# Mean layer of a graph network: edge features split in half tiles, residual and bias formed on POOL

## The chip, the cores and the metric

The kernel runs on one core of one Trainium2 chip. The metric is device microseconds (us) of one execution. Before the change it took 2363.88 us (median of 3 runs, 2360.2 to 2365.95).

## The reference

Four graph layers follow each other over 3125 nodes of 128 features and 103,125 edges that are sorted by target node. The change is in the second one, the mean layer, which the kernel overlaps with work for the fourth:

```
# layer 1 (mean aggregation), then residual and layer norm
agg = segment_sum(x[col], row, n) / max(degree, 1)
h   = relu(agg @ W1.T + b1)
x   = layernorm(x + h @ W2.T + b2)
# layer 3 needs, per target node, the sum of its edges' 16 features
segment_sum(edge_attr_16, dst, n)
```

## The kernel before

The nodes are held as 25 tiles of 128 (`TILES`), and a strip is 5 tiles (`STRIPS` = 5). `k.C` holds the matrix of edge counts, so that an aggregation is a matrix product. `mean_layer` (L877) does 5 strips x 25 tiles = 125 steps `(i, t)`. In each, PE transposes five 128x128 blocks of `k.C` (`turn`, L1115), ACT copies them from PSUM to `cs` (L1085), and PE adds 8 matmuls into `pA` and `pD` (`add`, L1129).

The edge sums run in the same steps. An edge tile has 36 chunks of 128 edges (`EC`), cut into 4 batches of 9 chunks (`EB`); there are 100 batches, in the steps t = 1 to 6 and 11 to 24 of each strip (`with_batch`). For batch n:

- SP waits for `lower` of batch n-2, loads an address register and issues the DMA of `feat[n % 2]`, 72 KB (`load_batch`, L940); before the first batch of a tile it also issues the targets `dst` (L931).
- The f32 features are split into three bf16 parts in `eparts[n % 2]`. ACT casts the high part (`high_part`, L1073, needs the DMA and the end of batch n-2 on PE); POOL subtracts it, giving `left` (L1049); ACT casts the middle part (`middle_part`, L1077); POOL subtracts that, giving the low part (L1051).
- DVE compares targets with places and writes the one-hot matrices `hot[n % 2]` (`match`, L1010, needs the end of batch n-2). It reads two operands from SBUF, as do POOL's subtractions.
- PE does 9 matmuls (`batch`, L1142), which need `hots` and `low` of batch n. After each fourth batch DVE takes the sum out of PSUM (L1015, L1016).

ACT, PE, DVE and SP run their queues in the order of the steps. ACT's and PE's work for a strip's end hangs in the next strip's steps: DVE's `mean(i-1)` at t = 1 (L974, a reciprocal of 4.15 us at L976, L978), PE's `first` after t = 2 (L1152), ACT's `hidden` at t = 4 (L1063), PE's `second` after t = 6 (L1158), DVE's `finish(i-1)` behind the match of t = 6. `finish` adds the bias b2 to the PSUM result (L986), then the residual x (L988), both into y, and normalizes (L707 to L714). The x of a strip is loaded by SP at t = 12 (L961), the old strip is stored at t = 20 (L946).

Of the kernel before, what the change touches and what calls it, by code (L numbers as in the profile page):

```python
# [26 lines left out]
P = 128  # L27
N_NODES = 3125
N_EDGES = 103125
D = 128  # L30
# [48 lines left out]
LIVE = N_NODES + 1  # L79
RISE = 2.0 ** 40  # L80
CHUNKS = ((0, 6), (6, 12), (12, 18), (18, TILES))
V_PARTS = tuple((lo, lo + PERIOD) for lo in range(0, TILES, PERIOD))
# [55 lines left out]
def mid(row, n):  # L138

    p, w = row.shape  # L140
    return row.unsqueeze(1).broadcast_to([p, n, w])
# [735 lines left out]
def mean_layer(nc, a, k, parts):  # L877
# [3 lines left out]
    with ExitStack() as ctx:  # L881
# [5 lines left out]
        cs = m.sb("cs", [P, CS, SW], BF16)  # L887
        x, y, out = (m.sb(n, [P, STRIP, D], F32) for n in ("x", "y", "out"))
        sq, w = out, out[:, 0:2, :]
# [3 lines left out]
        places = m.sb("places", [P, P, EG], BF16)  # L893
        feat, left = m.sb("feat", [P, 2, EB, FE], F32), m.sb("left", [P, 2, EB, FE], F32)
        dst, key = m.sb("dst", [P, 2, EC], I32), m.sb("key", [P, 2, EC + 1], BF16)
        eparts = m.sb("eparts", [P, 2, EB, ER], BF16)
        hot = m.sb("hot", [P, 2, (EB + 1) // EG, P, EG], BF16)
# [6 lines left out]
            m.sem(n) for n in ("turned", "cs_ready", "cs_used", "agg_out", "deg_out"))  # L904
        aggT_ready, p1, hT_ready, p2, added = (m.sem(n) for n in ("aggT_ready", "p1", "hT_ready", "p2", "added"))
        chain, var, std, normed, stored = (m.sem(n) for n in ("chain", "var", "std", "normed", "stored"))
        feat_in, dst_in = ([m.sem(f"{n}{s}") for s in (0, 1)] for n in ("feat_in", "dst_in"))
        high, lower, middle, low = (m.sem(n) for n in ("high", "lower", "middle", "low"))
# [9 lines left out]

        def part_of(n, part):
            return eparts[:, n % 2, :, 1 + FE * part:1 + FE * (part + 1)]  # L920

        with nc.Block() as block:
            @block.sync
            def _(sp):
# [8 lines left out]

                def load_batch(n):
                    t, b = divmod(n, HB)
                    if b == 0:
                        load_dst(t)
                    if n > 1:
                        sp.wait_ge(lower, n - 1)
                    sp.dma_start(feat[:, n % 2], a["edge_attr"][bass.ds(edges(t), EC * P), :]  # L940
                                 .rearrange("(p c) f -> p c f", c=EC)[:, b * EB:(b + 1) * EB, :]
                                 ).then_inc(feat_in[n % 2], 16)

# [8 lines left out]
                sp.dma_start(b2[:, :], a["b2_1"].partition_broadcast(P)).then_inc(consts, 16)  # L952
                load_batch(0)
                load_batch(1)
                sp.dma_start(x[:, :, :], strip_of(k.x1, 0)).then_inc(loaded, 16)
                for n, (i, t) in enumerate(with_batch):
                    if n + 2 < len(with_batch):
                        load_batch(n + 2)
# [9 lines left out]
            def _(dve):  # L968
# [11 lines left out]
                def finish(i):  # L980
                    link = Chain(dve, chain, i * (1 + NORM_LINKS))
                    dve.wait_ge(p2, i + 1)
                    if i:
                        dve.wait_ge(normed, i)
                    dve.wait_ge(loaded, i * 16 + 16)
# [10 lines left out]
                    normalize(link, act_link, dve, y[:, :, :], sq[:, :, :], st, out[:, :, :]).then_inc(normed, 1)  # L996
                    assert link.n == 1 + NORM_LINKS, link.n

# [43 lines left out]
            def _(pool):  # L1042
                pool.iota(places[:, :, :], [[1, P], [0, EG]], base=0, channel_multiplier=0,
                          allow_small_or_imprecise_dtypes=True).then_inc(made, 1)
                for n in range(len(with_batch)):
                    pool.wait_ge(high, n + 1)
                    if n > 1:
                        pool.wait_ge(low, n - 1)
                    pool.tensor_tensor(left[:, n % 2], feat[:, n % 2], part_of(n, 0), ALU.subtract).then_inc(lower, 1)  # L1049
                    pool.wait_ge(middle, n + 1)  # L1050
                    pool.tensor_tensor(part_of(n, 2), left[:, n % 2], part_of(n, 1), ALU.subtract).then_inc(low, 1)  # L1051
                pool.wait_ge(cs_used, STRIPS * TILES)
# [5 lines left out]
            def _(act):  # L1058
# [9 lines left out]

                def high_part(n):
                    act.wait_ge(feat_in[n % 2], 16 * (n // 2 + 1))  # L1070
                    if n > 1:
                        act.wait_ge(chunks, n - 1)
                    nc.scalar.activation(part_of(n, 0), feat[:, n % 2], ACT.Copy).then_inc(high, 1)  # L1073

                def middle_part(n):
                    act.wait_ge(lower, n + 1)
                    nc.scalar.activation(part_of(n, 1), left[:, n % 2], ACT.Copy).then_inc(middle, 1)  # L1077
# [26 lines left out]
            def _(pe):  # L1104
# [30 lines left out]
                def batch(n):  # L1135
                    t, b = divmod(n, HB)
                    pe.wait_ge(hots, n + 1)
                    pe.wait_ge(low, n + 1)
                    if t and b == 0:
                        pe.wait_ge(sums_out, t)  # L1140
                    for c in range(EB):
                        ins = pe.matmul(pE[:, :], hot[:, n % 2, c // EG, :, c % EG], eparts[:, n % 2, c, :],  # L1142
                                        start=b == 0 and c == 0, stop=b == HB - 1 and c == EB - 1,
                                        skip_group_check=True)
                    ins.then_inc(chunks, 1)
# [1472 lines left out]
```

## Time and profile before

| | |
|---|---|
| time, median of 3 runs | 2363.88 us |
| profiled execution, span | 2364.9 us, mean granted TensorE clock 0.898 |
| engines over the whole span | PE 76%, DVE 61%, ACT 43%, POOL 40% |
| mean layer, first hot to last output | about 569 to 857 us |
| its steps, 570 to 838 us | PE busy 222.96 us, DVE 178.95, POOL 152.23, ACT 144.64 of 268 |

Each row of a timeline gives the start in us from the span's start, how long the instruction took, its engine, line, operation, output and input tile, and in brackets how long the engine had been idle and what ended that. "SPq" rows are DMA issues by SP; a DMA's landing is later. A table of windows gives the busy time of each engine in a stretch, with the granted clock (1.00 is 2.4 GHz, 0.50 is 1.2 GHz). In a group of lines, the numbers behind the bar are busy us, mean ns of one instruction, and the idle time of the engine just before them, with what ended it. Where an engine waited for two things, the one that is named isn't always the one that came last: the ends of both have to be compared.

### The profile page before, as it was taken

The numbers are of one execution on the slowest core, as the hardware profiler recorded it, in microseconds if no ns is written. First come the engines' busy times: TensorE is split into PE (matmuls) and PEld (weight loads), VectorE is DVE, ScalarE is ACT, GpSimd is POOL, SyncE is SP. The second block draws the span as 40 slices with busy tenths as digits, with TensorE's granted clock in tenths as the row PEclk, the third lists the DMA queues.
The fourth block names the chain that finished last, engine by engine and source line by source line (L and its number), as shares of the span: only waits on it lengthen the run. The fifth ranks groups of instructions, "written<-read, shape, count | busy, mean of one in ns | idle before, by whom it ended". The sixth has DMA issues, their size and how long they took to land. (4 is left out here: it accounts for less than half of the span.)

```text
span 2364.9 us, 63669 instructions
## 1 busy us (share of the span) xinstructions
PE 1804.0 (76%) x24559; PEld 1430.7 (60%) x24674; DVE 1433.6 (61%) x2262; ACT 1017.2 (43%) x1655; POOL 956.2 (40%) x664
## 2 busy tenths in 40 slices
PE   4699998744888832788888886249907999999996
PEld 1699998733556522677777776149904555555553
DVE  6799999535676743799999997548760111110213
ACT  1455555302555511888889896237600110110100
POOL 0899889314555530888888770000031000000000
PEclk9899999956999966899999999669958999999998
DMA  1100000021111112111111100410020000000001
GB/s 50 38 13 14 14 12 11 11 66 44 34 43 42 42 33 63 35 41 37 37 37 37 37 33 7 116 60 12 12 85 18 9 7 8 6 9 4 15 14 43
DMA packets 93856, 73.97 MB, mean 31 GB/s; under 512 B 22862, under 2 KB 84055, under 8 KB 93505
## 3 DMA queue, kind: packets, MB, share of 16 engines
q1 hardware_dynamic: 90279, 67.88, 10.0%
q0 software_dynamic: 3328, 2.56, 0.6%
q8 instruction: 182, 2.98, 0.5%
q14 instruction: 67, 0.55, 0.1%
HBM read 51.57 MB, written 18.84 MB: 30 GB/s over the span
## 5 line engine op out<-in xcount | busy, mean ns | idle before, releaser
L2136 ACT ACTIVATE branch_mask<-branch_row,att_att 128x3126 bf16<-128x3126 f32 (+1 forms) x208 | 460.8, 2288 | 45.9 <-DMA branch_row<-dst_row 31.4
L429 POOL DMA_INDIRECT swp_slab<-records,e_rows x100 | 335.7, 3357 | 90.8 <-POOLq L110 56.1
L2213 PE MATMUL branch_acc<-branch_v,branch_mask 128*128 128x102 bf16 (+1 forms) x5000 | 297.8, 213 | 62.4 <-DVE branch_mask L2163 41.1
L2169 DVE TENSOR_TENSOR branch_mask<-branch_mask,k_C 128x3126 bf16<-128x3126 bf16 (+1 forms) x208 | 313.8, 1556 | 16.4 <-ACT branch_mask L2136 15.7
L2213 PEld LDWEIGHTS branch_acc<-branch_v,branch_mask 128*128 128x128 bf16 (+1 forms) x5000 | 254.6, 100 | 89.1 <-DVE branch_mask L2163 45.4
L2471 DVE SCALAR_TENSOR_TENSOR sage_y<-sage_pO,k_rdeg,sage_b 128x128 f32<-128x128 f32 x125 | 34.6, 344 | 449.7 <-PE sage_pO L2398 449.4
L862 PE MATMUL sage_pA<-k_C,k_x_parts 128*128 x2175 | 299.3, 294 | 4.9 <-issue 1.0
L862 PEld LDWEIGHTS sage_pA<-k_C,k_x_parts 128*128 x2250 | 166.4, 98 | 133.4 <-issue 3.3
L353 PE MATMUL swp_pw<-swp_key_hot,swp_low_hot 128*128 128x100 bf16 x1568 | 201.2, 217 | 31.8 <-DVE swp_key_hot L347 31.6
L2452 ACT ACTIVATE sage_aggT<-sage_pA 128x640 f32<-128x640 f32 x25 | 17.6, 703 | 463.5 <-PE sage_pO L2398 368.4
L353 PEld LDWEIGHTS swp_pw<-swp_key_hot,swp_low_hot 128*128 128x128 bf16 x1568 | 180.4, 119 | 39.2 <-DVE swp_key_hot L347 38.1
L356 PE MATMUL swp_pw<-swp_key_hot,swp_low_hot 128*128 128x50 bf16 x3136 | 201.3, 192 | 0.0
L862 PE MATMUL sage_pA<-k_C,sage_parts 128*128 x1460 | 198.3, 293 | 2.2
L356 PEld LDWEIGHTS swp_pw<-swp_key_hot,swp_low_hot 128*128 128x128 bf16 x3136 | 192.1, 117 | 0.0
L2202 PE MATMUL branch_acc<-branch_v,k_C 128*128 128x51 bf16 x5000 | 165.9, 187 | 28.9 <-POOL branch_v L2111 16.9
L347 DVE TENSOR_TENSOR swp_key_hot<-swp_key_hot,swp_tab 128x400 bf16<-128x400 bf16 x588 | 178.8, 358 | 0.0
L2202 PEld LDWEIGHTS branch_acc<-branch_v,k_C 128*128 128x128 bf16 x5000 | 143.5, 97 | 41.6 <-issue 22.4
L862 PEld LDWEIGHTS sage_pA<-k_C,sage_parts 128*128 x1500 | 110.1, 97 | 87.6
L1973 PE MATMUL scaled_acc<-scaled_tab,scaled_e 128*128 (+1 forms) x1250 | 142.1, 277 | 9.2 <-DVE scaled_e L1950 9.2
L1010 DVE TENSOR_TENSOR mean_hot<-mean_places,mean_key 128x1280 bf16<-128x1280 bf16 x100 | 120.9, 1222 | 46.4 <-PE mean_pE L1142 46.1
L1973 PEld LDWEIGHTS scaled_acc<-scaled_tab,scaled_e 128*128 128x128 f32 x1250 | 141.9, 194 | 9.5 <-issue 9.5
L842 POOL CAST k_x_parts<-post_out 128x640 bf16<-128x640 f32 x5 | 3.6, 716 | 347.6 <-DVE post_out L714 347.6
(307 smaller groups left out, 3218.0 us busy)
## 6 DMA issues: line engine op xcount, KB each, us to landing
branch_row<-dst_row SPq DMA_DIRECT2D x24, 384.0 KB
mean_feat<-in_edge_attr SPq DMA_DIRECT2D x100, 72.0 KB, 1.9
branch_row<-dst_row SPq DMA_DIRECT2D x8, 411.0 KB
sage_edges<-edgeT SPq DMA_DIRECT2D x25, 127.5 KB
table<-lin_tab SPq DMA_DIRECT2D x5, 340.0 KB, 5.3
branch_tab<-table SPq DMA_DIRECT2D x8, 212.5 KB
att_sums<-branch_mask SPq DMA_DIRECT2D x8, 212.5 KB, 2.3
post_sums<-att_sums SPq DMA_DIRECT2D x5, 340.0 KB, 3.4
```

The costliest lines, as they stand in the source:

```text
L347: ins = dve.tensor_tensor(key_hot[:, :, 1 + f], key_hot[:, :, 0], weight.broadcast_to(shape), ALU.mult)
L353: pe.matmul(out[:, 0:2 * KEYS], low_hot, key_hot[:, 0:2, :].rearrange("p f j -> p (f j)"), start=start, stop=False, skip_group_check=True)
L356: ins = pe.matmul(out[:, KEYS:2 * KEYS], low_hot, key_hot[:, f, :], start=False, stop=f == PARTS, skip_group_check=True)
L429: pool.indirect_dma_start(slab[:, t % 2, j * ROW:(j + 1) * ROW, :].rearrange("p e f -> p (e f)"), None, k.records, bass.IndirectOffsetOnAx ...
L862: ins = pe.matmul(pA[:, lo:hi], parts[:, part, bass.ds(s * STRIP + t, 1), :].rearrange("p a f -> p (a f)"), k.C[:, bass.ds(s * STRIP + t, ...
L1010: dve.tensor_tensor(hot[:, n % 2], places[:, :, :].unsqueeze(1).broadcast_to(shape), of.unsqueeze(2).broadcast_to(shape), ALU.is_equal).th ...
L1973: ins = pe.matmul(acc_tile(j, c), e[:, slot, c * P:(c + 1) * P], one(tab, s), start=isinstance(s, int) and s == 0 and c % per_bank == 0, s ...
L2136: nc.scalar.activation(mask[:, slot(e, s), cols(lo, hi)], row[:, cols(lo, hi)], ACT.Relu, bias=g.att[:, 1, bass.ds(h + s * heads, 1)], sca ...
L2169: dve.tensor_tensor(at[:, cols(lo, hi)], at[:, cols(lo, hi)], k.C[:, s, cols(lo, hi)], ALU.min).then_inc(masked, 1)
L2202: pe.matmul(block_of(e, t)[:, half:2 * half], k.C[:, s, t * P:(t + 1) * P], v[:, s, 2, :, :].rearrange("p r c -> p (r c)"), start=s == 0 a ...
L2213: ins = pe.matmul(block_of(e, t)[0:wide.stop - wide.start], mask[:, slot(e, s), wide], v[:, s, 0:2, :, :].rearrange("p x r c -> p (x r c)" ...
L2471: ins = dve.scalar_tensor_tensor(out=y[:, c, :], in0=pO[:, c * D:(c + 1) * D], scalar=k.rdeg[:, i * STRIP + c:i * STRIP + c + 1], in1=b[:, ...
```

## The change

Within `mean_layer`, four things change.

- Features are fetched and split in groups of two batches (18 chunks, 144 KB): 50 groups in place of 100 batches, so 50 DMAs of features, 100 ACT casts and 100 POOL subtractions of 128x288 in place of 100, 200 and 200 of 128x144. DVE's matches and PE's batches stay 100 of 9 chunks.
- The remainder overwrites `feat` in place (the tile `left` is gone), so the DMA of group g waits for `low` of group g-2 and no longer for `lower`. `feat` has 2 buffers, `eparts` has 3 (`GROUPS`). ACT's high part of group g waits for batch 2(g-3)+1.
- The order is another: ACT casts `high_part(g + 2)` at the odd batch of group g and `middle_part(g + 1)` at the even one, with `high_part(0)`, `high_part(1)` and `middle_part(0)` ahead of the first step. POOL does `lower_part(g + 1)` and then the low part of g.
- POOL adds b2 to x in place (`add_bias`, after group 8 of every 10), and DVE's `finish` has one addition where it had two; y is gone, and x is normalized in place. SP's load of x waits for `normed` in place of `added`.

```diff
-                    if n > 1:
-                        sp.wait_ge(lower, n - 1)
+                    if g > 1:
+                        sp.wait_ge(low, g - 1)
...
-                        sp.wait_ge(added, i)
+                        sp.wait_ge(normed, i)
                         sp.dma_start(x[:, :, :], strip_of(k.x1, i)).then_inc(loaded, 16)
...
-                    link(dve.tensor_tensor(y[:, :, :], flatB[:, 0:SW].rearrange("p (t f) -> p t f", f=D),
-                                           mid(b2[:, :], STRIP), ALU.add))
-                    dve.tensor_tensor(y[:, :, :], y[:, :, :], x[:, :, :], ALU.add).then_inc(added, 1)
+                    dve.wait_ge(residual, i + 1)
+                    dve.tensor_tensor(x[:, :, :], flatB[:, 0:SW].rearrange("p (t f) -> p t f", f=D), x[:, :, :],
+                                      ALU.add).then_inc(added, 1)
...
+                def add_bias(i):
+                    pool.wait_ge(consts, 16 * 4)
+                    pool.wait_ge(loaded, i * 16 + 16)
+                    pool.tensor_tensor(x[:, :, :], x[:, :, :], mid(b2[:, :], STRIP), ALU.add).then_inc(residual, 1)
+
+                def lower_part(g):
+                    pool.wait_ge(high, g + 1)
+                    pool.tensor_tensor(feat[:, g % 2], feat[:, g % 2], part_of(g, 0),
+                                       ALU.subtract).then_inc(lower, 1)
+
+                lower_part(0)
+                for g in range(2 * TILES):
+                    if g + 1 < 2 * TILES:
+                        lower_part(g + 1)
+                    pool.wait_ge(middle, g + 1)
+                    pool.tensor_tensor(part_of(g, 2), feat[:, g % 2], part_of(g, 1), ALU.subtract).then_inc(low, 1)
+                    if g % (HB * STRIP // 2) == HB * STRIP // 2 - 2:
+                        add_bias(g // (HB * STRIP // 2))
...
+                def high_part(g):
+                    act.wait_ge(feat_in[g % 2], 16 * (g // 2 + 1))
+                    if g >= GROUPS:
+                        act.wait_ge(chunks, 2 * (g - GROUPS + 1))
+                    nc.scalar.activation(part_of(g, 0), feat[:, g % 2], ACT.Copy).then_inc(high, 1)
...
                 high_part(0)
+                high_part(1)
+                middle_part(0)
...
-                        middle_part(batch_of[i, t])
-                        if batch_of[i, t] + 1 < len(with_batch):
-                            high_part(batch_of[i, t] + 1)
+                        g, odd = divmod(batch_of[i, t], 2)
+                        if odd and g + 2 < 2 * TILES:
+                            high_part(g + 2)
+                        elif not odd and g + 1 < 2 * TILES:
+                            middle_part(g + 1)
...
-                    pe.wait_ge(low, n + 1)
+                    pe.wait_ge(low, n // 2 + 1)
```

## Rows read from the trace of the kernel before

**Rows 1.** Windows, batches of t = 11 to t = 24 in each strip, with columns.
```profile
core 0: us, PE busy (x) PEld busy (x) DVE busy (x) ACT busy (x) POOL busy (x), PEclk, DMA share, GB/s
592.34:620.72 28.38, 22.77 (x288) 16.20 (x286) 17.17 (x22) 15.82 (x40) 20.76 (x26) 1.00 0.17 37
646.49:673.58 27.09, 22.93 (x288) 16.02 (x287) 18.39 (x24) 15.26 (x38) 21.13 (x26) 1.00 0.25 61
702.29:731.38 29.09, 24.45 (x287) 17.47 (x288) 18.42 (x24) 16.07 (x40) 19.07 (x27) 0.94 0.23 57
757.14:784.26 27.12, 22.94 (x288) 16.10 (x288) 18.25 (x24) 15.25 (x38) 21.27 (x27) 1.00 0.25 61
811.38:837.37 25.99, 22.60 (x281) 16.15 (x282) 16.54 (x22) 15.13 (x37) 19.27 (x26) 1.00 0.24 60
```

**Rows 2.** Timeline, two batches in steady state.
```profile
605.77 0.39 PE L1142 MATMUL mean_pE<-mean_eparts,mean_hot 128*128 128x49 bf16 x9
606.20 1.49 DVE L1010 TENSOR_TENSOR mean_hot<-mean_places,mean_key 128x1280 bf16<-128x1280 bf16 x1 [0.84 <-PE mean_pE L1142]
606.53 1.48 POOL L1051 TENSOR_TENSOR mean_eparts<-mean_left,mean_eparts 128x144 bf16<-128x144 f32 x1 [0.44 <-ACT mean_eparts L1077]
607.97 0.45 POOL L1049 TENSOR_TENSOR mean_left<-mean_feat,mean_eparts 128x144 f32<-128x144 f32 x1
608.16 0.39 PE L1142 MATMUL mean_pE<-mean_eparts,mean_hot 128*128 128x49 bf16 x9 [0.62 <-POOL mean_eparts L1051]
608.59 0.83 DVE L1010 TENSOR_TENSOR mean_hot<-mean_places,mean_key 128x1280 bf16<-128x1280 bf16 x1 [0.89 <-PE mean_pE L1142]
609.17 0.33 SPq L940 DMA_DIRECT2D mean_feat<-in_edge_attr  x1
...
611.05 0.33 ACT L1073 ACTIVATE mean_eparts<-mean_feat 128x144 bf16<-128x144 f32 x1 [0.54 <-DMA mean_feat<-in_edge_attr]
```

**Rows 3.** Timeline, PE's spacing of two batches that nothing holds up.
```profile
576.48 0.39 PE L1142 MATMUL mean_pE<-mean_eparts,mean_hot 128*128 128x49 bf16 x9
...
578.08 0.39 PE L1142 MATMUL mean_pE<-mean_eparts,mean_hot 128*128 128x49 bf16 x9
```

**Rows 4.** Groups of lines, 566 to 858 us.
```profile
L1010 DVE TENSOR_TENSOR mean_hot<-mean_places,mean_key 128x1280 bf16<-128x1280 bf16 x100 | 120.9, 1222 | 46.4 <-PE mean_pE L1142 46.1
L1051 POOL TENSOR_TENSOR mean_eparts<-mean_left,mean_eparts 128x144 bf16<-128x144 f32 x100 | 93.7, 937 | 91.8 <-ACT mean_eparts L1077 91.8
...
L1049 POOL TENSOR_TENSOR mean_left<-mean_feat,mean_eparts 128x144 f32<-128x144 f32 x100 | 61.2, 612 | 27.5 <-ACT mean_eparts L1073 27.0
...
L1073 ACT ACTIVATE mean_eparts<-mean_feat 128x144 bf16<-128x144 f32 x100 | 32.8, 328 | 60.5 <-DMA mean_feat<-in_edge_attr 40.3 <-PE mean_pE L1142 19.7
...
L1098 ACT ACTIVATE mean_aggT<-mean_pA 128x640 f32<-128x640 f32 x5 | 3.5, 704 | 2.0 <-PE mean_pD L1129 2.0
```

**Rows 5.** Timeline, a POOL subtraction of 640 elements in the layer before.
```profile
559.61 1.39 POOL L843 TENSOR_TENSOR gin_rest<-gin_out,x_parts 128x640 f32<-128x640 f32 x1
```

**Rows 6.** DMA issues, 566 to 840 us: count, KB each, median us to landing.
```profile
mean_feat<-in_edge_attr SPq DMA_DIRECT2D x100, 72.0 KB, 1.9
...
x<-mean_out SPq DMA_DIRECT2D x4, 320.0 KB, 2.6
```

**Rows 7.** Timeline, the handover from ACT's cast to POOL's subtraction.
```profile
601.25 0.33 ACT L1073 ACTIVATE mean_eparts<-mean_feat 128x144 bf16<-128x144 f32 x1 [2.95 <-DMA mean_feat<-in_edge_attr]
...
601.66 0.45 POOL L1049 TENSOR_TENSOR mean_left<-mean_feat,mean_eparts 128x144 f32<-128x144 f32 x1 [1.75 <-ACT mean_eparts L1073]
```

**Rows 8.** Timeline, the first two operations of DVE's finish.
```profile
638.60 0.82 DVE L986 TENSOR_TENSOR mean_y<-mean_pB,mean_b 128x640 f32<-128x640 f32 x1 [3.89 <-PE mean_pB L1158]
...
639.45 0.82 DVE L988 TENSOR_TENSOR mean_y<-mean_y,mean_x 128x640 f32<-128x640 f32 x1
```

**Rows 9.** Windows, strip's last batch to t = 6, the shortest and longest of four.
```profile
620.72:636.71 15.99, 12.92 (x149) 9.46 (x150) 12.22 (x13) 9.04 (x22) 7.94 (x13) 1.00 0.12 25
673.58:691.32 17.74, 14.28 (x150) 10.24 (x150) 12.64 (x13) 9.11 (x21) 7.94 (x12) 0.90 0.12 27
```

More of the change, by code:

```diff
@@ L80 @@
 RISE = 2.0 ** 40
+GROUPS = 3
 CHUNKS = ((0, 6), (6, 12), (12, 18), (18, TILES))
@@ L887, in mean_layer @@
         cs = m.sb("cs", [P, CS, SW], BF16)
-        x, y, out = (m.sb(n, [P, STRIP, D], F32) for n in ("x", "y", "out"))
+        x, out = (m.sb(n, [P, STRIP, D], F32) for n in ("x", "out"))
         sq, w = out, out[:, 0:2, :]
@@ L893, in mean_layer @@
         places = m.sb("places", [P, P, EG], BF16)
-        feat, left = m.sb("feat", [P, 2, EB, FE], F32), m.sb("left", [P, 2, EB, FE], F32)
+        feat = m.sb("feat", [P, 2, EC // 2, FE], F32)
         dst, key = m.sb("dst", [P, 2, EC], I32), m.sb("key", [P, 2, EC + 1], BF16)
-        eparts = m.sb("eparts", [P, 2, EB, ER], BF16)
+        eparts = m.sb("eparts", [P, GROUPS, EC // 2, ER], BF16)
         hot = m.sb("hot", [P, 2, (EB + 1) // EG, P, EG], BF16)
@@ L904, in mean_layer @@
             m.sem(n) for n in ("turned", "cs_ready", "cs_used", "agg_out", "deg_out"))
-        aggT_ready, p1, hT_ready, p2, added = (m.sem(n) for n in ("aggT_ready", "p1", "hT_ready", "p2", "added"))
+        aggT_ready, p1, hT_ready, p2, added, residual = (
+            m.sem(n) for n in ("aggT_ready", "p1", "hT_ready", "p2", "added", "residual"))
         chain, var, std, normed, stored = (m.sem(n) for n in ("chain", "var", "std", "normed", "stored"))
-        feat_in, dst_in = ([m.sem(f"{n}{s}") for s in (0, 1)] for n in ("feat_in", "dst_in"))
+        feat_in = [m.sem(f"feat_in{s}") for s in (0, 1)]
+        dst_in = [m.sem(f"dst_in{s}") for s in (0, 1)]
         high, lower, middle, low = (m.sem(n) for n in ("high", "lower", "middle", "low"))
@@ L917, in mean_layer, with part_of @@
         assert len(with_batch) == TILES * HB
-        def part_of(n, part):
-            return eparts[:, n % 2, :, 1 + FE * part:1 + FE * (part + 1)]
+        def part_of(g, part):
+            return eparts[:, g % GROUPS, :, 1 + FE * part:1 + FE * (part + 1)]
         with nc.Block() as block:
@@ L980, in finish @@
                 def finish(i):
[L981 removed]
+                    link = Chain(dve, chain, i * NORM_LINKS)
                     dve.wait_ge(p2, i + 1)
[L983 to L988 removed]
+                    dve.wait_ge(residual, i + 1)
+                    dve.tensor_tensor(x[:, :, :], flatB[:, 0:SW].rearrange("p (t f) -> p t f", f=D), x[:, :, :],
+                                      ALU.add).then_inc(added, 1)
                     dve.wait_ge(added, i + 1)
@@ L995, in finish @@
                         dve.wait_ge(stored, i * 16)
-                    normalize(link, act_link, dve, y[:, :, :], sq[:, :, :], st, out[:, :, :]).then_inc(normed, 1)
-                    assert link.n == 1 + NORM_LINKS, link.n
+                    normalize(link, act_link, dve, x[:, :, :], sq[:, :, :], st, out[:, :, :]).then_inc(normed, 1)
+                    assert link.n == NORM_LINKS, link.n
                 def match(n):
@@ L1044, in _ @@
                           allow_small_or_imprecise_dtypes=True).then_inc(made, 1)
[L1045 to L1051, printed above, removed]
+                def add_bias(i):
[14 more added lines that the diff above has]
+                        add_bias(g // (HB * STRIP // 2))
                 pool.wait_ge(cs_used, STRIPS * TILES)
@@ L1067, in root, with middle_part @@
                     nc.scalar.activation(st[:, 2, :], st[:, 1, :], ACT.Sqrt).then_inc(std, 1)
[L1069 to L1077, printed above, removed]
+                def high_part(g):
[3 more added lines that the diff above has]
+                    nc.scalar.activation(part_of(g, 0), feat[:, g % 2], ACT.Copy).then_inc(high, 1)
+                def middle_part(g):
+                    act.wait_ge(lower, g + 1)
+                    nc.scalar.activation(part_of(g, 1), feat[:, g % 2], ACT.Copy).then_inc(middle, 1)
                 high_part(0)
+                high_part(1)
+                middle_part(0)
                 act.wait_ge(consts, 16 * 4)
@@ L1141, in batch @@
                     for c in range(EB):
-                        ins = pe.matmul(pE[:, :], hot[:, n % 2, c // EG, :, c % EG], eparts[:, n % 2, c, :],
+                        ins = pe.matmul(pE[:, :], hot[:, n % 2, c // EG, :, c % EG], eparts[:, n // 2 % GROUPS, n % 2 * EB + c, :],
                                         start=b == 0 and c == 0, stop=b == HB - 1 and c == EB - 1,
```

20 lines of the change are left out of this document (10 added, 10 removed).

## The prediction, made before the changed kernel was run

> **What bounds the kernel now.** I read the page first (the mean layer is a stage of its own, some 290 of 2364.9 us), then windows of that stage, then its timeline. The changed code runs nowhere else, so only the mean layer can move, unless it leaves the clock or a queue in another state for the next stage.
>
> In the stretch t = 11 to 24 of each strip, which has 14 batches and so 13 spacings, the five strips take 28.38, 27.09, 29.09, 27.12 and 25.99 us, 137.7 in all [rows 1]: 2.12 us a batch, 4.24 a pair. PE, when nothing holds it, needs 1.60 us for a step with a batch [rows 3], 3.20 a pair, and is busy 22.6 to 24.5 us of 26 to 29 [rows 1]. So PE is not quite the bound. The timeline shows what is [rows 2]. The batch at 605.77 ends; DVE's next hot starts 0.43 later and takes 1.49 us. POOL's low part starts at 606.53 and takes 1.48 us where the same kind of subtraction takes 0.45 at 607.97: it ends at 608.01, which is 0.32 behind the hot's end at 607.69. PE's batch follows at 608.16. The reader should see that POOL stands still while DVE runs an operation with two SBUF operands, and that every batch then costs 0.43 + hot + 0.32 + 0.15 us: 2.39 with the 1.49 us hot, 1.72 with the 0.83 us one (608.16 to 609.88 by this sum). The two kinds of hot alternate, and their mean is 1.22 [rows 4]. PE's waits are booked partly on the hot, but the low part ends last.
>
> The supply of features is close behind: ACT's high part waited 40.3 us in all for DMA and 19.7 for PE's batches, by two buffers [rows 4].
>
> **The change: the pace of a group.** The terms of one subtraction of 288 elements: 0.45 us for 144 [rows 2], 1.39 for 640 [rows 5], so by the straight line 0.72; bounds 0.45 (all fixed) and 0.90 (all by size). ACT's cast: 0.33 for 144 and 0.70 for 640 [rows 4], so 0.44; bounds 0.33 and 0.66. The DMA: low or left end to issue 0.75 (608.42 to 609.17), issue to ACT's start 1.88 [rows 2]; a 320 KB DMA lands 0.7 later than a 72 KB one [rows 6], so 144 KB lands 0.2 later, 2.08; bounds 1.88 and 2.58. ACT to POOL 0.08 [rows 7].
>
> Saved work: POOL's subtractions were 200 x 0.45 = 90 us unblocked and become 100 x 0.72 = 72, so 18 us less need of the port that DVE's hots also use; ACT saves 100 x 0.66 - 100 x 0.44 = 22 us. Neither is an engine's full load, so this counts only through what each step waits for.
>
> What decides is the new order. The DMA of group g waits for low(g-2); POOL must do lower(g) before low(g-1); lower(g) needs high(g), which needs the DMA. So one round, low(g-2) to low(g-1), holds a whole DMA and two subtractions in series: 0.75 + 2.08 + 0.44 + 0.08 + 0.72 + 0.72 = 4.79 us for two batches, against 4.24 now. Before, the DMA of batch n waited only for left(n-2), and one such round (0.75 + 1.88 + 0.33 + 0.08 + 0.45 = 3.49) served two batches. The three `eparts` buffers don't help: `feat` has two, and the position of lower ahead of low makes them act as one. ACT waits in its queue at high(g), and the copy `cs` of the next step stands behind it, so PE is starved by the same round.
>
> Then the hots. Measured from the end of a high part (H), copy 0.69 and PE's step put the next batches at H + 2.1 and H + 3.7, the hots that follow them at H + 2.6 and H + 4.2 (0.2 later where DVE first takes sums out). The next lower part is due at H + 4.9. A 1.49 us second hot runs until 5.7 or 5.9 and holds it; a 0.83 one is over or nearly so. A held 144-element operation ended 0.32 behind the hot, 0.13 less than its own 0.45, so a held one of 288 ends about 0.59 behind. The second hot is long in the two groups of one tile and short in the two of the next. Working four groups in a row gives rounds of 4.8, 5.6, 5.1 and 4.8: mean 5.1. I take 5.1 us.
>
> The Trainium skill (SBUF — State Buffer, "SBUF: two separate sides") says that whichever of a two-input DVE operation and a GpSimd operation starts first has the shared ports for the whole instruction and the other fully blocks. The trace agrees, with 1.48 us for a 0.45 us operation. By a strict reading, with the blocked one starting only then, it would need its full 0.72 behind the hot; that would add 0.13 in about half the rounds, 2 us over the layer.
>
> **The change: the sum.** In t = 11 to 24, the second pair follows the first after about 3.4 us (its features were fetched during the strip's tail, but its lower part meets two hots), then five rounds of 5.1 lead to t = 23, then 1.9 to t = 24: 30.8 us. The last strip has no lower part after group 49 and saves 1.9. Five strips: 5 x 30.8 - 1.9 = 152.1, against 137.7: +14.4.
>
> Between a strip's last batch and t = 6 (15.99 to 17.74 us now [rows 9]) DVE's mean with its long reciprocal sets the pace, and the DMA round fits under it. ACT no longer waits there for the batch before last, but larger POOL operations can hold the mean's last product by up to 0.7: -0.4 for each of 4, -1.5; bounds -4 and +3.
>
> `finish` loses its first addition, 638.60 to 639.45, 0.85 us [rows 8]. The hot for t = 11 stands behind it, and at the end the next layer does: 5 x -0.85 = -4.3. The residual is long there: add_bias has about 1.4 us [rows 5] and comes after group 8 of 10, in the 3.3 us in which POOL waits for the next high part; if that cover is gone, it costs up to 1.4 x 5 = 7. Behind its wait for x, loaded ten steps earlier, stand POOL's lower parts. SP's load of x now waits for the end of normalizing, which is also what frees the hot for t = 11, so the feature DMA behind it isn't late; and the 320 KB are in flight before the next feature DMA.
>
> At the start ACT does high(0), high(1) and middle(0) before its first copy, which waits for a lower part under the second hot: some 2.5 us later, most of which the first rounds would have cost anyway: +0.5; bounds 0 and +2.5.
>
> Sum: +14.4 - 1.5 - 4.3 + 0.5 = +9.1 on the span of 2364.9: 2374.0. The median of the runs lies 1.0 below the span of the profiled execution, so the time is **2373 us**, 0.4% more.
>
> **Rivals.**
>
> A. *The round is shorter and the gain remains.* If a subtraction had nearly its fixed cost only, 0.45, and nothing were added to landing or cast, the round would be 0.75 + 1.88 + 0.33 + 0.08 + 0.90 = 3.94, and the hots would set about 4.1 (3.2 of PE with held POOL in between). Then t = 11 to 24 gives -3, the rest -5: 2356. The 640-element row speaks against it; it decides in favour of faster below a round of about 4.5. Chance 0.08.
>
> B. *The round matters less*, because the second hots come in a better phase and the finish and boundary give more: a round of 4.8 and -3 at the boundaries: 25 rounds x 0.3 = 7.5 less, 1.5 less: 2364. Nothing excludes it, since the phase of hot and lower part is a difference of tenths. Chance 0.25.
>
> C. *TensorE's clock.* PE would be busy about 3.2 of 5.1 us, 63%, where it is 84% now. In the third strip the granted clock was 0.94 though PE was busy 24.45 of 29.09 us, and that strip took 2.0 us more than the second and the fourth [rows 1]. If it falls to 1.2 GHz that often or oftener in each strip, 5 to 8 such losses cost 10 to 16 us: 2383 to 2389. Of the Trainium skill (TensorE: Matmul & The Clock Gate, "HAM oscillation — how this bites in real kernels") I take that waits for DMA between bursts of matmuls can let the clock fall again and again; the waits here would be some 1.9 us a round. Chance 0.12.
>
> D. *The new DMA wait isn't last* since something else has replaced it, the change not doing what it says (copies and batches run as before, POOL's low part still behind the hot): 4.24 a pair, and only the finish and boundary gains: 2364 - 5 = 2359. Chance 0.05.
>
> **How the numbers follow.** My forecast has 0.50 (its own range, rounds of 4.9 to 5.4, 2367 to 2381), A 0.08, B 0.25, C 0.12, D 0.05. The range leaves out A and the far end of C: 2361 to 2388. About 7 us, 0.3%, is what a measurement of this kernel can tell from no change. Slower by more: 0.40 of the forecast, 0.05 of B, C whole and a rest of longer landings, together 0.60. Faster by more: A's half and a little of D, 0.07. Between: 0.33.
>
> **What would show it.** SP's issue of the features 0.75 behind the end of every low part, ACT's high part released by the DMA in nearly every group of t = 11 to 24, idle time of ACT there 1.5 to 2.5 us a round, PE's copies waited for; low to low 4.8 to 5.6 us; windows of t = 11 to 24 near 31 us, the last near 29. POOL operations of 0.72 unheld. finish 0.85 shorter with the hot of t = 11 earlier by that. Wrong would be: high parts that find their features landed (then the order isn't the bound), subtractions near 0.5, or windows of 27 us and less; a granted clock under 0.9 in the windows speaks for C.

## The result and the profile after

The changed kernel took 2396.11 us (median of 4 runs, 2387.75 to 2399.65) against 2363.68 (4 runs, 2360.2 to 2365.95): ratio 1.0134, 95% interval 1.0101 to 1.0166. The forecast was 2373 us, 9 us slower; it is 32 us slower. The profiled execution has a span of 2390.7 us (2364.9 before).

The mean layer alone, from POOL's first instruction in it to the end of DVE's last, took 292.4 us before and 322.0 after: +29.5. The profile of before entered the layer 4.7 us later (564.24 against 559.59), so the layers before it hide a part of the difference between the two spans. What follows the layer took 1508.2 and 1509.1 us. The loss that the two profiles show is all in the layer. The profiled execution of the changed kernel took 2392.63 us, 3.5 less than its median; that is a part of why the spans differ by 26 us and the medians by 32.

The strips' stretches, from the starts of PE's batches, all strips summed:

| stretch | before | after | difference | forecast |
|---|---|---|---|---|
| layer's start to first batch | 10.6 | 14.2 | +3.6 | +0.5 with the next row |
| first strip, t = 1 to 6 | 10.4 | 8.7 | -1.7 | |
| t = 11 to 24, five strips | 137.7 | 152.6 | +14.9 | +14.4 |
| t = 6 to 11, five strips | 48.6 | 55.6 | +7.0 | -3.4 (four times finish) |
| t = 24 over the boundary to t = 6, four times | 65.8 | 72.2 | +6.4 | -1.5 |
| last batch to the layer's end | 19.3 | 18.6 | -0.7 | -0.9 |
| sum | 292.4 | 322.0 | +29.5 | +9.1 |

The windows of t = 11 to 24, to be held against [rows 1], with the same columns:

```profile
591.50:622.00 30.50, 23.37 (x288) 17.96 (x287) 16.65 (x22) 12.33 (x24) 11.54 (x13) 0.94 0.12 30
652.10:682.70 30.60, 23.41 (x288) 17.86 (x287) 19.64 (x24) 12.36 (x24) 12.12 (x13) 0.94 0.19 51
714.50:746.70 32.20, 23.60 (x287) 18.04 (x288) 20.17 (x24) 12.13 (x23) 13.91 (x13) 0.95 0.17 45
775.00:806.10 31.10, 21.99 (x289) 17.03 (x287) 19.46 (x24) 12.40 (x24) 11.48 (x13) 1.00 0.19 51
834.70:862.90 28.20, 21.68 (x281) 16.80 (x282) 18.03 (x22) 11.45 (x21) 11.78 (x12) 1.00 0.17 45
```

ACT and POOL are busy for a fifth to nearly a half less than before in each (12.3 against 15.8 us, 11.5 against 20.8 in the first), and each stretch is longer. Less work on an engine was not what was wanted here. The timeline of the changed kernel shows one round (two batches) in steady state:

```profile
665.91 5.39 SPq L943 DMA_DIRECT2D mean_feat<-in_edge_attr  x2
...
667.46 1.49 DVE L1010 TENSOR_TENSOR mean_hot<-mean_places,mean_key 128x1280 bf16<-128x1280 bf16 x1 [0.77 <-PE mean_pE L1157]
667.96 0.46 ACT L1084 ACTIVATE mean_eparts<-mean_feat 128x288 bf16<-128x288 f32 x1 [2.40 <-DMA mean_feat<-in_edge_attr]
668.31 0.68 ACT L1098 ACTIVATE mean_cs<-mean_pT 128x640 bf16<-128x640 bf16 x1
668.49 1.04 POOL L1052 TENSOR_TENSOR mean_feat<-mean_feat,mean_eparts 128x288 f32<-128x288 f32 x1 [3.32 <-ACT mean_eparts L1084]
...
669.05 0.45 PE L1130 MATMUL mean_pT<-mean_identb,k_C 128*128 128x128 bf16 x5 [1.62 <-ACT mean_cs L1098]
...
669.50 0.72 POOL L1060 TENSOR_TENSOR mean_eparts<-mean_feat,mean_eparts 128x288 bf16<-128x288 f32 x1
```

The DMA is issued at 665.91, 0.74 us behind the end of a low part. 2.05 later ACT's high part starts, for which ACT stood 2.40 us. POOL's lower part follows, held by the hot until 668.95 and ending 0.58 behind it; then the low part, which releases the next DMA (the second of the two issues in the first row, at 670.97). One round is 5.06 us. PE's transposes wait 1.62 us for the copy that stands behind the high part in ACT's queue.

The groups of the layer, to be held against [rows 4]:

```profile
L1052 POOL TENSOR_TENSOR mean_feat<-mean_feat,mean_eparts 128x288 f32<-128x288 f32 x50 | 50.8, 1017 | 197.6 <-ACT mean_eparts L1084 197.6
L1060 POOL TENSOR_TENSOR mean_eparts<-mean_feat,mean_eparts 128x288 bf16<-128x288 f32 x50 | 44.7, 894 | 0.0
...
L1084 ACT ACTIVATE mean_eparts<-mean_feat 128x288 bf16<-128x288 f32 x50 | 22.8, 455 | 119.6 <-DMA mean_feat<-in_edge_attr 119.0 <-PE mean_pE L1157 0.6
```

ACT's idle time before the high part, put down to the DMA, grew from 40.3 to 119.0 us. In exchange its wait for PE's batches fell from 19.7 to 0.6: the third buffer of parts does what it should, and it is worth less than what the DMA takes.

The end of a strip is where the forecast was wrong. The changed kernel from the last batch of the first strip (622.00) to the first of the second (628.92):

```profile
622.00 0.40 PE L1157 MATMUL mean_pE<-mean_eparts,mean_hot 128*128 128x49 bf16 x9
...
622.83 0.46 ACT L1084 ACTIVATE mean_eparts<-mean_feat 128x288 bf16<-128x288 f32 x1 [2.58 <-DMA mean_feat<-in_edge_attr]
...
623.19 0.68 ACT L1113 ACTIVATE mean_aggT<-mean_pA 128x640 f32<-128x640 f32 x1
...
624.52 0.45 PE L1130 MATMUL mean_pT<-mean_identb,k_C 128*128 128x128 bf16 x5 [2.12 <-ACT mean_cs L1098]
624.80 1.72 PE L1144 MATMUL mean_pA<-mean_cs,x_parts 128*128 128x320 bf16 x6
...
627.97 0.83 DVE L981 TENSOR_TENSOR mean_aggT<-mean_aggT,mean_hT 128x640 f32<-128x640 f32 x1
...
628.72 4.02 DVE L1010 TENSOR_TENSOR mean_hot<-mean_places,mean_key 128x1280 bf16<-128x1280 bf16 x3
...
628.92 0.40 PE L1157 MATMUL mean_pE<-mean_eparts,mean_hot 128*128 128x49 bf16 x9
```

ACT stands 2.58 us for features that no batch needs yet, and the copies that open the next strip come late. But the hot of t = 2 stands in DVE's queue behind `mean`, and it starts at 628.72, 6.7 us after the last batch; before, it started 6.4 us after it (620.72 to 627.12):

```profile
627.12 3.48 DVE L1010 TENSOR_TENSOR mean_hot<-mean_places,mean_key 128x1280 bf16<-128x1280 bf16 x3
```

So this wait of ACT is nearly hidden. The next one is not: at t = 4 ACT stands at a high part again, and `hidden` and the next copy are behind it.

```profile
634.98 0.45 ACT L1084 ACTIVATE mean_eparts<-mean_feat 128x288 bf16<-128x288 f32 x1 [3.04 <-DMA mean_feat<-in_edge_attr]
...
635.34 0.77 ACT L1074 ACTIVATE mean_hT<-mean_pB,mean_b 128x640 f32<-128x640 f32 x1
...
636.76 0.45 PE L1130 MATMUL mean_pT<-mean_identb,k_C 128*128 128x128 bf16 x5 [1.50 <-ACT mean_cs L1098]
```

From the hot of t = 2 to the batch of t = 6 the four boundaries took 40.2 us before and 46.3 after. And behind the batch of t = 6 of the second strip:

```profile
640.05 0.40 PE L1157 MATMUL mean_pE<-mean_eparts,mean_hot 128*128 128x49 bf16 x9
642.38 0.46 ACT L1084 ACTIVATE mean_eparts<-mean_feat 128x288 bf16<-128x288 f32 x1 [3.76 <-DMA mean_feat<-in_edge_attr]
...
643.47 0.45 PE L1130 MATMUL mean_pT<-mean_identb,k_C 128*128 128x128 bf16 x5 [3.02 <-ACT mean_cs L1098]
...
643.76 1.33 PE L1173 MATMUL mean_pB<-mean_wT,mean_hT 128*128 128x128 f32 x10
...
645.13 0.82 DVE L987 TENSOR_TENSOR mean_x<-mean_pB,mean_x 128x640 f32<-128x640 f32 x1 [8.17 <-PE mean_pB L1173]
```

ACT stands at a high part whose features aren't needed for several steps. Behind it in its queue is the copy of t = 7, which PE's transposes of t = 8 wait for; and `second`, which releases DVE's whole `finish`, stands behind those transposes in PE's queue. `finish` starts 5.08 us after the batch; before, it did so 1.89 us after it (636.71 to 638.60).

### The profile page after: what moved, and what is told of

It is laid out like the page before. It is cut to its first block and busy times, and to the rows that moved or that the text cites. A ratio compares the mean times of both kernels' runs of the same rounds, so it can differ in the third digit from the quotient of the medians.

```text
span 2390.7 us, 63140 instructions
## 1 busy us (share of the span) xinstructions
PE 1819.0 (76%) x24674; PEld 1447.6 (61%) x24674; DVE 1437.0 (60%) x2257; ACT 1000.7 (42%) x1555; POOL 898.2 (38%) x569
## 5 line engine op out<-in xcount | busy, mean ns | idle before, releaser
L2151 ACT ACTIVATE branch_mask<-branch_row,att_att 128x3126 bf16<-128x3126 f32 (+1 forms) x208 | 460.7, 2289 | 46.9 <-DMA branch_row<-dst_row 30.7
L2184 DVE TENSOR_TENSOR branch_mask<-branch_mask,k_C 128x3126 bf16<-128x3126 bf16 (+1 forms) x208 | 313.1, 1553 | 17.4 <-ACT branch_mask L2151 16.9
L2467 ACT ACTIVATE sage_aggT<-sage_pA 128x640 f32<-128x640 f32 x25 | 17.6, 704 | 464.5 <-PE sage_pO L2413 368.4
L2217 PEld LDWEIGHTS branch_acc<-branch_v,k_C 128*128 128x128 bf16 x5000 | 144.4, 97 | 44.2 <-issue 24.5
L1010 DVE TENSOR_TENSOR mean_hot<-mean_places,mean_key 128x1280 bf16<-128x1280 bf16 x100 | 125.9, 1273 | 71.9 <-PE mean_pE L1157 71.0
L2178 DVE SCALAR_TENSOR_TENSOR branch_mask<-branch_row,branch_low,k_C 128x3126 bf16<-128x3126 f32 x40 | 143.9, 3597 | 0.0
```

The lines of the kernel that those rows point to most:

```text
L1010: dve.tensor_tensor(hot[:, n % 2], places[:, :, :].unsqueeze(1).broadcast_to(shape), of.unsqueeze(2).broadcast_to(shape), ALU.is_equal).th ...
L2151: nc.scalar.activation(mask[:, slot(e, s), cols(lo, hi)], row[:, cols(lo, hi)], ACT.Relu, bias=g.att[:, 1, bass.ds(h + s * heads, 1)], sca ...
L2178: dve.scalar_tensor_tensor(out=at[:, 0:LIVE], in0=row[:, :], scalar=low[:, s // PERIOD, bass.ds(h, 1)], in1=k.C[:, s, 0:LIVE], op0=ALU.is_ ...
L2184: dve.tensor_tensor(at[:, cols(lo, hi)], at[:, cols(lo, hi)], k.C[:, s, cols(lo, hi)], ALU.min).then_inc(masked, 1)
L2217: pe.matmul(block_of(e, t)[:, half:2 * half], k.C[:, s, t * P:(t + 1) * P], v[:, s, 2, :, :].rearrange("p r c -> p (r c)"), start=s == 0 a ...
```

## The experiments

The theory after the two traces: the loss comes from the round in which one DMA and two subtractions stand in series for each group (theory 1), and at the strip's boundary the round acts through ACT's queue. The rivals: the size of the operations, which the hots hold longer (theory 2); the residual part (theory 3); and the clock.

**The order alone turned.** In POOL's queue the low part of g goes ahead of the lower part of g+1; nothing else is touched.

```diff
                 lower_part(0)
                 for g in range(2 * TILES):
-                    if g + 1 < 2 * TILES:
-                        lower_part(g + 1)
                     pool.wait_ge(middle, g + 1)
                     pool.tensor_tensor(part_of(g, 2), feat[:, g % 2], part_of(g, 1), ALU.subtract).then_inc(low, 1)
+                    if g + 1 < 2 * TILES:
+                        lower_part(g + 1)
```

> The changed kernel with one order turned: POOL does the low part of group g first and the lower part of g+1 behind it. Sizes, buffers and waits stay. Theory 1 (the round: low(g-2), DMA of g, high(g), lower(g), low(g-1) in series, about 5 us for two batches): low(g) no longer stands behind a DMA, so a round serves two groups; t = 11 to 24 falls from about 30.5 us a strip to 26 to 28, ACT's wait for features from 106 us to under 50, and the time to 2350 to 2365 us. Theory 2 (the size: operations of 288 elements that the hots hold longer, and 144 KB loads): nothing much changes, 2385 to 2400 us.

2346.07 us, ratio to the kernel before 0.9916 (0.9895 to 0.9936): 50 us faster than the changed kernel by moving two lines, and faster than before by 0.8%. That is below the 2350 to 2365 I expected: t = 11 to 24 takes 22.6 to 25.6 us a strip, 119.4 in all, where I expected 130 to 140. The waits of the layer's steps, changed kernel and then this one (who waited for whom, total us, times, longest):

```profile
ACT mean_eparts L1084 <- DMA mean_feat<-in_edge_attr: 105.8, 39, 4.3
...
PE mean_pT L1130 <- ACT mean_cs L1098: 61.6, 38, 3.2
```

```profile
ACT mean_eparts L1084 <- DMA mean_feat<-in_edge_attr: 21.1, 15, 3.0
...
PE mean_pT L1130 <- ACT mean_cs L1098: 17.0, 21, 2.2
```

Sizes and buffers are the same in both, so theory 2 can't carry the loss.

**The same wait and order in small batches.** The kernel before, with the two edits of order and wait only. `lower_part(n)` stands for the four lines that are taken out of the loop.

```diff
                     if n > 1:
-                        sp.wait_ge(lower, n - 1)
+                        sp.wait_ge(low, n - 1)
...
+                lower_part(0)
                 for n in range(len(with_batch)):
-                    pool.wait_ge(high, n + 1)
-                    if n > 1:
-                        pool.wait_ge(low, n - 1)
-                    pool.tensor_tensor(left[:, n % 2], feat[:, n % 2], part_of(n, 0), ALU.subtract).then_inc(lower, 1)
+                    if n + 1 < len(with_batch):
+                        lower_part(n + 1)
                     pool.wait_ge(middle, n + 1)
```

> The kernel before, batches and loads of 9 chunks, with only the wait and the order of the change: the DMA of batch n waits for low(n-2) in place of lower, and POOL does lower(n+1) ahead of low(n). Theory 1: a round of 0.75 + 1.95 + 0.33 + 0.08 + 0.45 + 0.45 = 4.0 us, with holds 4.2 to 4.6, now serves one batch of 9 chunks where 2.12 us was the pace: t = 11 to 24 takes 52 to 60 us a strip, the time 2500 to 2570 us. Theory 2 (what costs is the size of the operations and loads): 2363 to 2380 us.

2542.4 us (2 runs), ratio 1.0756 (1.0727 to 1.0786). t = 11 to 24 takes 260.6 us for 65 spacings: 4.01 us a batch, the sum of the unheld terms. A round costs 4.0 us with loads of one batch and 5.25 with loads of two (the changed kernel), so it is mostly a price for each load; half as many loads is why the changed kernel loses only 32 us and not 179. Its round in the timeline:

```profile
612.26 0.33 ACT L1078 ACTIVATE mean_eparts<-mean_feat 128x144 bf16<-128x144 f32 x1 [2.71 <-DMA mean_feat<-in_edge_attr]
...
612.67 0.45 POOL L1049 TENSOR_TENSOR mean_left<-mean_feat,mean_eparts 128x144 f32<-128x144 f32 x1 [3.07 <-ACT mean_eparts L1078]
613.08 0.45 POOL L1056 TENSOR_TENSOR mean_eparts<-mean_left,mean_eparts 128x144 bf16<-128x144 f32 x1
...
613.68 0.39 PE L1147 MATMUL mean_pE<-mean_eparts,mean_hot 128*128 128x49 bf16 x9 [2.22 <-POOL mean_eparts L1056]
```

**The DMA taken out of the round.** The changed kernel without the feature loads after the first two groups, so that the edge sums are formed of the wrong features; the high part waits for low(g-2) itself.

```diff
                     if g > 1:
-                        sp.wait_ge(low, g - 1)
+                        return
...
-                    act.wait_ge(feat_in[g % 2], 16 * (g // 2 + 1))
+                    act.wait_ge(feat_in[g % 2], 16)
+                    if g > 1:
+                        act.wait_ge(low, g - 1)
```

> The changed kernel without the feature DMAs after the first two groups (so the edge sums are formed of the wrong features); ACT's high part waits for low(g-2) in place of the DMA. Order, sizes and buffers stay. Theory 1: the round shrinks by 2.85 us to about 2.1 us plus what hots hold, below PE's 3.2 us for two batches; t = 11 to 24 takes 21 to 25 us, the time 2330 to 2350 us. Theory 2 (size of the operations under the port lock): still 28 us and more for t = 11 to 24, above 2375 us.

2336.05 us, ratio 0.9862 (0.9839 to 0.9886). t = 11 to 24: 115.6 us, 21.8 to 24.5 a strip. The order that costs so much with the DMA in it costs nothing without it. From the hot of t = 2 to t = 6 the four boundaries take 38.8 us, against 46.3 in the changed kernel. With no loads to wait for, this order is 10 us below the turned kernel: that bounds what faster loads could still give the changed order.

**ACT's high parts at the boundary moved on.** The changed kernel; the high part of t = 24 goes behind the copy of the next t = 0, that of t = 6 behind the copy of t = 8.

```diff
-                        if odd and g + 2 < 2 * TILES:
+                        if odd and t not in (FINISH, TILES - 1) and g + 2 < 2 * TILES:
                             high_part(g + 2)
...
+                    if t in (0, FINISH + 2) and (i or t):
+                        high_part((20 * i + (5 if t else -1)) // 2 + 2)
```

> The changed kernel with two of ten high parts of a strip moved on in ACT's queue: the one at t = 24 to behind the copy of t = 0, the one at t = 6 to behind the copy of t = 8. If ACT's queue, standing at a high part whose features haven't landed, is what lengthened the strip's boundary (t = 24 to 1, t = 6 to 11), these go back from 6.6 and 11.1 us to about 4.5 and 9.5 us while t = 11 to 24 stays at 30 to 31: 2378 to 2388 us. If the boundary grew for the lost clock or held DVE operations, it stays, 2392 to 2400 us.

2382.19 us, ratio 1.0065 (1.0044 to 1.0086), 14 us faster than the changed kernel. t = 6 to 11 falls from 55.6 to 43.7 us (and that is 4.9 below before: finish's gain comes out at last), and t = 11 to 24 stays at 152.7. t = 24 to 1 falls too, from 26.6 to 17.4, but t = 1 to 6 grows from 54.4 to 64.0, and from t = 24 over the boundary to t = 6 nothing is gained: 72.5 against 72.2. So the stall at t = 6 is ACT's queue, as stated, and its 11.9 us are the whole gain (the layer is 11.2 us shorter). The stall at t = 24 costs nothing by itself, since `mean` sets the time up to the hot of t = 2, and the round is the longer for its later start behind it.

**The residual part alone, on the kernel before.**

```diff
                     pool.tensor_tensor(part_of(n, 2), left[:, n % 2], part_of(n, 1), ALU.subtract).then_inc(low, 1)
+                    if n % 20 == 17:
+                        add_bias(n // 20)
...
-                    link(dve.tensor_tensor(y[:, :, :], flatB[:, 0:SW].rearrange("p (t f) -> p t f", f=D),
-                                           mid(b2[:, :], STRIP), ALU.add))
-                    dve.tensor_tensor(y[:, :, :], y[:, :, :], x[:, :, :], ALU.add).then_inc(added, 1)
+                    dve.wait_ge(residual, i + 1)
+                    dve.tensor_tensor(x[:, :, :], flatB[:, 0:SW].rearrange("p (t f) -> p t f", f=D), x[:, :, :],
+                                      ALU.add).then_inc(added, 1)
```

> The kernel before with only the residual part of the change: POOL adds b2 to x behind the low part of the third batch from the end of a strip, DVE's finish has one addition, SP's load of x waits for normed. Theory 1 has no part here; finish gives 0.85 us five times, and POOL's 1.54 us addition, put where the low part is what PE's batch waits for, takes about 1 us four times: 2359 to 2364 us. Theory 3 (the residual part caused some of the loss: a late x, a held POOL): above 2370 us.

2365.78 us, ratio 0.9995 (0.9983 to 1.0007): nothing. t = 6 to 11 falls by 3.4 us, as `finish` should give, and t = 11 to 24 grows by 8.2, twice the 4 I expected of it, so that the time lies just above the 2359 to 2364 I expected; t = 1 to 6 was 2.0 shorter. POOL's addition stands in front of a lower part here:

```profile
613.42 1.54 POOL L1046 TENSOR_TENSOR mean_x<-mean_x,mean_b 128x640 f32<-128x640 f32 x1
614.92 1.70 POOL L1052 TENSOR_TENSOR mean_left<-mean_feat,mean_eparts 128x144 f32<-128x144 f32 x1
```

The residual part doesn't cost what theory 3 needed (above 2370 us), in these small batches at least; the next run asks the same of the large ones.

**The turned kernel with the bias back on DVE.** `finish` has two additions on x, POOL none.

```diff
-                    dve.wait_ge(residual, i + 1)
+                    dve.wait_ge(loaded, i * 16 + 16)
                     dve.tensor_tensor(x[:, :, :], flatB[:, 0:SW].rearrange("p (t f) -> p t f", f=D), x[:, :, :],
-                                      ALU.add).then_inc(added, 1)
+                                      ALU.add).then_inc(residual, 1)
+                    dve.wait_ge(residual, i + 1)
+                    dve.tensor_tensor(x[:, :, :], x[:, :, :], mid(b2[:, :], STRIP), ALU.add).then_inc(added, 1)
...
-                    if g % (HB * STRIP // 2) == HB * STRIP // 2 - 2:
-                        add_bias(g // (HB * STRIP // 2))
```

> The order of POOL turned, and the bias added by DVE in finish as before, in place (two additions on x), none on POOL. If POOL's bias addition is hidden once a group's low part comes early, finish loses 0.85 us five times: about 4 us above the order alone, 2350 us, t = 6 to 11 near 9.7 us. If it stands on the path there, as in the kernel with the bias alone (t = 11 to 24 up by 1.6 us a strip), that comes off again: 2340 to 2346 us.

2347.5 us, ratio 0.9934 (0.9913 to 0.9956), against 0.9916 (0.9895 to 0.9936) with the bias on POOL. t = 6 to 11 is 3.5 us longer and t = 11 to 24 2.2 shorter: what DVE saves by giving the bias away, POOL's addition takes back by more than half. Whether the bias belongs on POOL at all, these runs can't tell.

**The turned kernel with the high parts moved on.** The edits of the two kernels above together.

> The order of POOL turned (low part first) and the two high parts of a strip's boundary moved on in ACT's queue. With the low part first the features have landed when ACT comes to them, so moving the high parts should bring little: 2340 to 2350 us, and t = 24 to 1 and t = 6 to 11 as with the order alone (4.4 and 8.8 us). If ACT still stands there for features, 2335 to 2342 us.

2344.73 us, ratio 0.9921 (0.9897 to 0.9944): the same as the order alone. Once the low part goes first, the features have landed when ACT comes to the boundary (1.2 us and more earlier, in all strips but the first), and there is nothing to move.

**Lead without larger operations.** First only a third buffer of parts in the kernel before:

```diff
-        eparts = m.sb("eparts", [P, 2, EB, ER], BF16)
+        eparts = m.sb("eparts", [P, 3, EB, ER], BF16)
...
-                    if n > 1:
-                        act.wait_ge(chunks, n - 1)
+                    if n > 2:
+                        act.wait_ge(chunks, n - 2)
```

> The kernel before with three buffers of bf16 parts in place of two, batches of 9 chunks. ACT's high part no longer waits for the batch before last (19.7 us of its waits before). If lead alone is what the turned kernel gains by, the time falls to 2345 to 2355 us. If in t = 11 to 24 the held low part is the bound, as the trace of before says, only t = 1 to 6 gets 1 to 2 us a strip shorter: 2356 to 2363 us, and t = 11 to 24 stays at 27 to 28 us.

2359.66 us, ratio 0.9981 (0.997 to 0.9992). t = 1 to 6 is 4.3 us shorter in all, t = 11 to 24 stays (136.6). The held low part was the bound there, as [rows 2] say. Then that buffer with the turned kernel's schedule, still in batches of 9 chunks (POOL does the low part of n and then the lower part of n+1, which the cut doesn't show):

```diff
-                        middle_part(batch_of[i, t])
-                        if batch_of[i, t] + 1 < len(with_batch):
-                            high_part(batch_of[i, t] + 1)
+                        if batch_of[i, t] + 1 < len(with_batch):
+                            middle_part(batch_of[i, t] + 1)
+                        if batch_of[i, t] + 2 < len(with_batch):
+                            high_part(batch_of[i, t] + 2)
```

> The kernel before, batches of 9 chunks and the tile left apart, with three buffers of parts and the turned kernel's schedule: ACT casts the middle part of batch n+1 and the high part of n+2 in the step of batch n, POOL does low(n) and then lower(n+1). No larger operations, no bias on POOL. If the turned kernel gains because the low part is ready a step ahead, so that a hot no longer delays PE, this one gains too: t = 11 to 24 falls to 23 to 26 us a strip, the time to 2342 to 2354 us. If it gains because 200 POOL subtractions became 100 larger ones, this one stays at 2356 to 2364 us.

2358.03 us, ratio 0.9985 (0.9968 to 1.0002). t = 11 to 24 takes 131.2 us: a third of the way from 137.7 to the turned kernel's 119.4. The time agrees with the second reading (size), the stretch, 26.2 us a strip, with neither. So a step's lead alone is not enough. Whether the rest of the turned kernel's gain comes from the halved number of POOL's operations, of ACT's casts or of the loads, the runs don't split: with the lead, ACT still waited for features, now ahead of its copies.

All stretches side by side, us, sums over the strips:

| kernel | layer | t 1 to 6 | t 6 to 11 | t 11 to 24 | t 24 to 1 |
|---|---|---|---|---|---|
| before | 292.4 | 59.9 | 48.6 | 137.7 | 16.3 |
| changed | 322.0 | 54.4 | 55.6 | 152.6 | 26.6 |
| changed, low first | 275.0 | 60.9 | 44.0 | 119.4 | 17.6 |
| changed, no reload | 266.4 | 54.5 | 43.3 | 115.6 | 20.3 |
| changed, high parts moved on | 310.8 | 64.0 | 43.7 | 152.7 | 17.4 |
| low first and high parts moved on | 272.8 | 56.6 | 43.3 | 121.3 | 19.8 |
| low first, bias on DVE | 274.4 | 59.1 | 47.5 | 117.2 | 17.9 |
| before, bias on POOL | 295.8 | 57.9 | 45.2 | 145.9 | 16.6 |
| before, wait and order changed | 469.5 | 103.9 | 57.0 | 260.6 | 17.4 |
| before, three buffers of parts | 285.9 | 55.6 | 47.5 | 136.6 | 16.5 |
| before, three buffers and lead | 290.3 | 58.7 | 49.9 | 131.2 | 17.2 |

A third buffer of features, with the change's order kept, wasn't tried.

## Why the prediction was right in direction and wrong in size

**The round: right.** Each term came out near its estimate: low end to issue 0.74 (0.75 forecast), the DMA 2.1 us to landing by the median (2.08), the cast 0.46 (0.44), an unheld subtraction 0.73 (0.72), a held one ending 0.58 behind the hot (0.59). The prediction's strict reading of what the Trainium skill says (SBUF — State Buffer, "SBUF: two separate sides"), a full 0.72 behind the hot, is not what the trace shows, and the measurement decides. The round from low part to low part was 5.25 us by the mean of 19 in steady state (5.1 forecast), and the stretch came to 152.6 us where the sum said 152.1. The turned order and the kernel without reloads show that this is the cause, and the small batches show its price with nothing else changed.

**The boundary: the step that failed.** I wrote that from the last batch to t = 6 "the DMA round fits under" DVE's mean, at -1.5 us, and counted finish's gain whole, at -3.4 of its -4.3 in t = 6 to 11. Measured: +6.4 and +7.0, 18 us of the 20 that the sum was short.

Up to t = 6, `mean` does set the pace, but only as far as the hot of t = 2 behind it: 25.6 us after the batches of t = 24 before, 25.9 after, all four boundaries summed. From there the round lengthens it: 46.3 us to t = 6 where it was 40.2, with ACT standing 2.1 to 3.8 us at each high part of t = 4. The low part of t = 5 was late for PE too (second strip: it ended at 638.24, the batch began at 638.34). With the loads out of the round this part takes 38.8 us (and all of t = 24 to 6 takes 66.9, where the changed kernel takes 72.2); with the high parts moved on in ACT's queue it takes 46.9. So the claim that the round fits under `mean` is what failed, by its loads, and ACT's stall at t = 24 itself cost next to nothing. One thing stays open: in the turned kernel ACT finds its features landed at t = 2 and t = 4 of every one of these strips, and the part still takes 43.8 us, 3.6 more than before.

From t = 6 to 11 it is ACT's queue. I had named this very mechanism one paragraph earlier for the steady state and did not ask it here: at t = 6 the high part stands ahead of the copy that PE's transposes, `second` and `finish` hang on. The kernel with the high parts moved on shows the cost, -11.9 us. Strip by strip this stretch was +2.0, +2.2, +3.1, -0.5 and +0.2 us against before. In the second and third, the loads there landed after 3.4 and 4.0 us, where the median is 2.1, so by estimate some 3 of the 7.0 us come from two slow landings that nothing here explains.

**The start: a term mis-sized.** The first copy was to be 2.5 us late and most of it to be absorbed, +0.5. The first batch was 3.6 us later in the layer, and 1.7 came back by t = 6: +1.9.

**Finish: right but covered.** With ACT's stalls gone, t = 6 to 11 is 4.6 to 4.9 us below before, somewhat more than 3.4. In the changed kernel the addition was shortened by 0.85 us five times, and in the four strips after the first, `finish` started 0.5 to 4.2 us later behind the batch of t = 6 than before.

**The clock (rival C): it fell as often, and cost less.** From the layer's first batch to its last, the granted clock fell to half 8 times in the changed kernel and 2 times before, the 5 to 8 losses that I gave this rival. Three of them lie in t = 11 to 24 (the windows show 0.94, 0.94, 0.95, 1.00 and 1.00), and there I had given it 10 to 16 us. The round explains that stretch to within 0.5 us, so the lower clock fell into time in which PE waited anyway. Four lie between t = 24 and t = 6. The kernel with the high parts moved on has one there, and takes 72.5 us where the changed one takes 72.2. The last lies in t = 6 to 11 of the third strip, where `second` took 2.41 us at half clock against 1.33, on the way to `finish`. No kernel here takes the clock alone away, so its own part in the +13.4 at the strips' ends stays open; the 1.1 us of `second` is what can be named.

**Rivals A, B and D** fell: no round below 4.7 us in steady state, ACT's high parts released by the DMA in all of them, SP's issue 0.75 us behind the low part by the median.

The range, 2361 to 2388, left out the measured 2396 because it was built from doubts about the round, the best known term, while the boundary, where nothing of the trace was like the changed order, had -4 to +3, and finish's gain had no bound for ACT's queue. The range also left out rival D's 2359 without saying so. One reading was loose and changed no sum: the hot at 606.20 starts 0.43 us after the start of the batch at 605.77, not after its end.

## What to carry to other kernels

When a buffer's release moves to a later step, write down the ring from release to release with all that stands in it, queue order included, and count how many units of work it serves; then ask whether turning two instructions in one in-order queue takes the DMA out of it (here that was worth 50 us, and made of a loss of 1.3% a gain of 0.8%). A wait in a queue has to be priced at each place where it stands, not only in steady state: what is behind it there may be the head of a long chain. Loads twice as large halved the number of rounds and made each only 1.2 us longer (4.0 to 5.25). Work moved to an engine that is idle on average pays nothing if it stands ahead of what the next step waits for: the bias on POOL gave 3.4 us in one stretch and took 8.2 in another.

## What the runs showed of the hardware that I had not expected

- Feature loads of 144 KB landed after 2.0 to 4.0 us (median 2.1), those of 72 KB before after 1.75 to 4.12 (median 1.9). The two longest waits at t = 6, 3.41 and 4.07 us from issue to cast, came with no other load that I could find in flight; they are open.
- Between the layer's first batch and its last, the granted clock fell to half (1.2 GHz) 2 times before, 8 times in the changed kernel, 4 times in the turned one and in the one without reloads, 3 times with the high parts moved on, never with three buffers of parts alone, and 21 times with small batches and the DMA in the round. The last is the one in which PE stands most (179 us of 439). Otherwise the drops don't follow that time: 3 drops with PE standing for 63 us (high parts moved on), 4 with 22 us (no reloads), 8 with 66 us (changed). None of the runs says what they follow.
- POOL's addition of a row that is broadcast over 5 tiles takes 1.54 us for 640 elements when nothing holds it, where a subtraction without broadcast took 1.39 [rows 5].
